# Cross-attention with a routed expert layer: attention in four steps of two head pairs, transposes and projection pieces in three shared PSUM banks

## The reference, cut to what matters

```python
# x, ctx: (32, 256, 256); mask: (32, 256); 16 heads of 64; 32 experts, hidden 64
h = layernorm(x)
q, k, v = h @ Wq, ctx @ Wk, ctx @ Wv
dots = q k^T * 64 ** -0.5, masked by mask and causally
x = x + softmax(dots) @ v @ Wo + bo
z = layernorm(x)
e = argmax(z @ router_w.T + router_b)          # one expert a token
x = x + relu(relu(z @ w1[e] + b1[e]) @ w2[e] + b2[e])
```

## Time and profile before

| | |
|---|---|
| median of the runs | 1570.09 us (1568.24 to 1631.78, 3 runs) |
| profiled execution | 1570.3 us, its span 1567.5 us |
| mean granted TensorE clock | 0.984 |
| instructions | 45480 |

### The profile page before, as it was taken

The page is one execution under the profiler, slowest core; times in us unless marked ns, Lnnn a source line. Parts: engine busy times, 40 slices in busy tenths (PEclk is TensorE's granted clock), DMA queues, the critical chain, the costliest instruction groups (busy, mean ns, idle before and its releaser), DMA issues.

```text
span 1567.5 us, 45480 instructions
## 1 busy us (share of the span) xinstructions
PE 1486.6 (95%) x14041; PEld 1248.9 (80%) x14042; DVE 1220.2 (78%) x5247; ACT 990.6 (63%) x3113; POOL 345.1 (22%) x508
## 2 busy tenths in 40 slices
PE   7899999999999999999999999999999999975884
PEld 6788888888888888888888888888888888864663
DVE  5777887888888888878888888888788888765663
ACT  5566666666666666666666666666666666643663
POOL 3212111111111111111111111111111111113776
PEclk9999999999999999999999999999999999997997
DMA  9543000000000000000000000000000000004761
GB/s 298 102 145 103 28 27 28 21 28 28 21 28 21 28 21 28 27 28 21 28 28 21 28 21 28 21 28 27 28 21 28 28 21 21 13 16 137 204 182 28
DMA packets 70399, 77.69 MB, mean 50 GB/s; under 512 B 11351, under 2 KB 64221, under 8 KB 70369
## 3 DMA queue, kind: packets, MB, share of 16 engines
q1 hardware_dynamic: 62546, 60.37, 14.0%
q0 software_dynamic: 7680, 16.93, 2.9%
q10 hardware_dynamic: 144, 0.03, 0.0%
HBM read 47.61 MB, written 33.88 MB: 52 GB/s over the span
## 4 chain that ended last, share of the span: by engine, by line
PE 81%; DVE 10%; issue 4%; ACT 1%; POOL 1%; DMA 1%; ACTq 1%; DVEq 0%; POOLq 0%; SPq 0%
PE psR L509 30%; PE psS L581 12%; PE psW L543 12%; PE psO L614 11%; PE psT L598 5%; PE psR L500 2%; PE psR L552 2%; DVE Sm L993 2%; DVE Sm L1010 2%; PE psS L1303 1%; PE psR L1293 1%; PE psT L1303 1%; DVE xn L830 1%; ACTq L1134 1%; PE psW L1282 1%
## 5 line engine op out<-in xcount | busy, mean ns | idle before, releaser
L739 ACT ACTIVATE Sm<-Sm,mneg 128x128 f32<-128x128 f32 (+1 forms) x1024 | 456.0, 449 | 364.1 <-DVE mneg L993 363.6
L993 DVE CUSTOM_DVE_ANT_0 Sm<-psS,MK 128x128 f32<-128x128 f32 (+1 forms) x1024 | 304.6, 354 | 110.4 <-PE psS L581 100.0
L581 PE MATMUL psS<-KT,QT 64*128 64x128 f32 (+1 forms) x2048 | 237.8, 351 | 21.0 <-DVE Sm L1010 18.6
L614 PE MATMUL psO<-PT,V 128*64 128x256 f32 (+1 forms) x2048 | 223.6, 339 | 1.3 <-ACT PT L730 1.3
L730 ACT ACTIVATE PT<-psT 128x768 f32<-128x768 f32 x256 | 204.5, 799 | 0.0
L581 PEld LDWEIGHTS psS<-KT,QT 64*128 64x128 f32 x2048 | 134.7, 187 | 77.9 <-issue 60.7
L739 ACT ACTIVATION_READ_ACCUMULATOR Sm<-Sm,mneg 128x1 f32 x1024 | 196.6, 192 | 0.0
L1010 DVE SCALAR_TENSOR_TENSOR Sm<-Sm,halve,rinv 128x512 f32<-128x512 f32 x256 | 193.3, 755 | 0.0
L448 POOL DMA_INDIRECT lists<-stg,lrow x64 | 67.8, 1059 | 560.0 <-DVE lrow L950 550.2
L614 PEld LDWEIGHTS psO<-PT,V 128*64 128x64 f32 x2048 | 124.5, 136 | 56.0 <-DVE OT_lo L1015 1.5
L598 PEld LDWEIGHTS psT<-ident,Sm 64*128 64x128 f32 x3072 | 138.2, 139 | 25.5 <-issue 1.7
(11 more groups left out here) (154 smaller groups left out, 2957.7 us busy)
## 6 DMA issues: line engine op xcount, KB each, us to landing
lists<-pad SPq DMA_DIRECT2D x8, 1560.0 KB, 12.9
XS<-lists SPq DMA_DIRECT2D x48, 260.0 KB
x_in<-in_x SPq DMA_DIRECT2D x32, 256.0 KB, 2.7
ctx_in<-in_ctx SPq DMA_DIRECT2D x32, 256.0 KB, 2.6
xr<-in_x SPq DMA_DIRECT2D x32, 256.0 KB, 2.6
W2R<-in_L_ffn_weights SPq DMA_DIRECT2D x1, 2048.0 KB
out<-Y,tok POOLq DMA_INDIRECT x96, 2.8
W2R<-in_L_xattn_Wv SPq DMA_DIRECT2D x2, 512.0 KB, 9.4
```

The costliest lines, as they stand in the source:

```text
L581: last = nc.tensor.matmul(psS[:, side, o:o + (it + 1) * P], QT[rows, p, it * P:(it + 1) * P], KT[rows, p, 0:(it + 1) * P], start=True, sto ...
L614: last = nc.tensor.matmul(psO[DH * side:DH * side + DH, t * P:N], V[:, t, DH * h:DH * h + DH], PT[:, blocks, :], start=(t == 0), stop=(t = ...
L739: nc.scalar.activation(v, v, ACT.Exp, bias=mneg[:, p % 2, k:k + 1], scale=-1.0, accum_out=rsum[:, p % 2, k:k + 1]).then_inc(s_exp, 1)
L993: nc.vector.tensor_tensor_reduce(out=Sm[:, p % 4, side, cols], in0=psS[:, side, cols], in1=MK[:, cols], scale=-SCALE, scalar=3e38, op0=ALU ...
```

## The change

A batch now has four steps, each for two pairs, a *quad*. In step s the PE does the scores of quad s+1 and the transposes of quad s, interleaved pair by pair, then the values of quad s-1 in one run of 16 instructions, then three to five pieces. psT, psW and the two psR banks are gone: psR has three banks, in which a quad's transposes lie (768 columns for each row half) and which the pieces then use in turn. psS has four banks, so that both pairs of a quad fit. Before the first transposes the PE waits for the reads of the last three pieces of the step before (`first_ready`), and it does so between the first and the second row block of the scores. A piece waits for the copy of the transposed probabilities from its bank, or for the read of the piece three before it.

The probabilities are copied in three parts of 512 columns into one of two buffers. `hi_o` and `lo_o` treat two pairs at once, 512 columns. The output projection is one piece, wo, at the end of step 0 of the next batch, in bank 2, and DVE reads it at the start of step 1. v2 is read by ACT instead of DVE. The router's stages are split: up to `tiles_run` in step 3 of the next batch, the rest in step 0 of the batch after that, and the rows are listed two batches later than their own instead of one. The mask's first-key scan is moved to step 0. In batch 0 DVE, not POOL, makes the low half of Wo. The first batches are written out for these offsets; the second phase only takes its banks from other names.

```diff
--- before.py
+++ after.py
...
-        PT = sb("PT", [P, 6, P])
+        PT = sb("PT", [P, 2, 3 * 512])
...
-        psS = ps("psS", 2)
-        psT = ps("psT", 2)
+        psS = ps("psS", 4)
         psO = ps("psO")
-        psW = ps("psW")
-        psR = [ps(f"psR{i}") for i in range(2)]
+        psR = ps("psR", 3)
...
+        QUADS = PAIRS // 2
+        PIECES = ((("v2", 0), ("xt", 1), ("wo", -1)),
+                  (("v3", 0), ("q0", 1), ("q1", 1), ("q2", 1)),
+                  (("x2", -1), ("k0", 1), ("lg", -1), ("k1", 1), ("v0", 1)),
+                  (("v1", 1), ("k2", 1), ("q3", 1), ("k3", 1)))
...
+            def iteration(b, prev, prev2, more, nxt=True):
+                if nxt:
+                    fold(b + 1)
+                if prev2:
+                    listed(b - 2)
+                if more:
+                    root1(b + 2)
+                if prev:
+                    root2(b - 1)
+                if nxt:
+                    lo_ctx(b + 1)
+                add_bias(b)
...
+            def scores(b, s, i, between=None):
+                p = 2 * s + i
                 for it, o in ((0, 0), (1, P)):
+                    if it and between:
+                        between()
                     for side in range(2):
                         rows = slice(DH * side, DH * side + DH)
-                        last = nc.tensor.matmul(psS[:, side, o:o + (it + 1) * P], QT[rows, p, it * P:(it + 1) * P],
+                        last = nc.tensor.matmul(psS[:, 2 * i + side, o:o + (it + 1) * P], QT[rows, p, it * P:(it + 1) * P],
                                                 KT[rows, p, 0:(it + 1) * P], start=True, stop=True)
                 last.then_inc(s_sc, 1)
 
+            def scores_may_start(b, s, first=False):
                 if not first:
+                    pe.wait_ge(s_sm, 8 * G(b, s) - 8)
+                pe.wait_ge(s_q, 4 * b + s + 1)
+                pe.wait_ge(s_k, 4 * b + s + 1)
+
+            def first_ready(b, s, prev, nxt):
+
+                pe.wait_ge(s_pn, 4 * G(b, s) - 2)
+                if s > 0:
+                    before = [(name, b + off) for name, off in pieces(s - 1, prev, nxt)]
+                elif prev:
+                    before = [(name, b - 1 + off) for name, off in pieces(QUADS - 1, prev, True)]
+                else:
+                    before = [(name, b) for name in FIRST]
+                if s > 0 or prev:
+                    pe.wait_ge(s_pt, 3 * G(b, s) - 3)
+                for name, at in before[-3:]:
+                    pe.wait_ge(*emptied(name, at))
+
+            def second_ready(b, s):
+
+                pe.wait_ge(s_pn, 4 * G(b, s))
+                pe.wait_ge(s_pt_half, G(b, s))
+
+            ring = psR[:].rearrange("p a n -> p (a n)")
+
+            def probs_t(b, s, i):
 
                 for side in range(2):
-                    for i, src in enumerate((2 * P, 0, P)):
-                        o = (3 * side + i) * DH
+                    for k, src in enumerate((2 * P, 0, P)):
+                        o = (6 * i + 3 * side + k) * DH
                         for h in range(2):
                             rows = slice(DH * h, DH * h + DH)
-                            last = nc.tensor.transpose(psT[:, h, o:o + DH], Sm[rows, p % 4, side, src:src + P],
-                                                       ident[rows, rows])
-                last.then_inc(s_pt_pe, 1)
-
+                            last = nc.tensor.transpose(ring[:, 768 * h + o:768 * h + o + DH],
+                                                       Sm[rows, 2 * (s % 2) + i, side, src:src + P], ident[rows, rows])
+                last.then_inc(s_pt_pe if i else s_pt_half, 1)
+
...
+                for s in range(QUADS):
+                    ahead = later(b, s + 1, nxt)
                     if ahead:
+                        if s == 0 and prev and not (isinstance(b, int) and b == 1):
+
+                            pe.wait_ge(s_pf, b - 1)
+                        scores_may_start(*ahead)
+                        scores(*ahead, 0, lambda: first_ready(b, s, prev, nxt))
+                        probs_t(b, s, 0)
+                        scores(*ahead, 1, lambda: second_ready(b, s))
+                        probs_t(b, s, 1)
+                    else:
+                        first_ready(b, s, prev, nxt)
+                        probs_t(b, s, 0)
+                        second_ready(b, s)
+                        probs_t(b, s, 1)
+                    if s > 0:
+                        values(b, s - 1, not prev and s == 1)
                     elif prev:
+                        values(b - 1, QUADS - 1)
+                    now = pieces(s, prev, nxt)
+                    for n, (name, off) in enumerate(now):
+                        if n < 3:
+                            pe.wait_ge(s_pt, 3 * G(b, s) - 2 + n)
                         else:
+                            pe.wait_ge(*emptied(now[n - 3][0], b + now[n - 3][1]))
+                        piece(name, b + off, psR[:, n % 3, :])
+                        if s == QUADS - 1 and prev and n == 1:
+                            ranks(b - 1, 8 * G(*ahead))
...
+            def probs_out(b, s):
+                act.wait_ge(s_pt_pe, G(b, s))
+                if not isinstance(b, int) or G(b, s) > 2:
+                    act.wait_ge(s_o_pe, G(b, s) - 2)
+                for k in range(3):
+                    nc.scalar.activation(PT[:, s % 2, 512 * k:512 * k + 512], psR[:, k, :], ACT.Copy).then_inc(s_pt, 1)
...
+            def hi_o(b, s):
+                act.wait_ge(s_o_pe, G(b, s))
+                if s == 0 and not (isinstance(b, int) and b == 0):
+
+                    act.wait_ge(s_wo_pe, b)
+                nc.scalar.activation(OTh[:, 2 * s:2 * s + 2, :].rearrange("p a n -> p (a n)"), psO[:, :], ACT.Copy
+                                     ).then_inc(s_o_hi, 1)
...
+                    exp(0, 0)
+                    probs_out(b, s)
+                    if s == 0:
+                        if prev:
+                            hi_o(b - 1, QUADS - 1)
+                            exp(0, 1)
+                            read("xt")
+                            exp(1, 0)
+                            exp(1, 1)
+                            read("v2")
...
+                    if s == 1:
+                        exp(0, 1)
+                        exp(1, 0)
+                        exp(1, 1)
+                        read("q0")
+                        if nxt:
+                            hi_ctx(b + 1)
+                        read("q1")
+                        hi_o(b, 0)
+                        read("q2")
+                    if s == 2:
+                        read("x2")
+                        exp(0, 1)
+                        exp(1, 0)
+                        read("k0")
+                        exp(1, 1)
+                        read("k1")
+                        hi_o(b, 1)
+                    if s == 3:
+                        exp(0, 1)
+                        exp(1, 0)
+                        exp(1, 1)
+                        read("k2")
+                        hi_o(b, 2)
+                        read("q3", "k3")
...
+                    if s == 0:
+                        route(prev2, b - 2, tiles_next)
+                        mask(0, 0)
+                        route(prev2, b - 2, rows_next)
+                        mask(0, 1)
+                        route(prev2, b - 2, rows_gap)
+                        mask(1, 0)
+                        route(prev2, b - 2, rows_near)
+                        mask(1, 1)
+                        if prev:
+                            lo_o(b - 1, QUADS - 1)
+                        route(prev2, b - 2, rows_all)
+                        if nxt:
+                            sum_ctx(b + 1)
+                        route(prev2, b - 2, rows_kept)
+                        norm(0)
+                        route(prev2, b - 2, row_places)
+                        read("xt") if prev else None
+                        route(prev2, b - 2, row_numbers)
+                        norm(1)
+                        route(prev2, b - 2, fills)
+                        if not prev:
+                            read("xt")
+                            lo_wo(0)
+                        if nxt:
+                            first_key(b + 1)
+                        if more:
+                            stats1(b + 2)
+                    if s == 1:
+                        if prev:
+                            residual(b - 1, bank_of(0, "wo", prev, nxt))
+                        mask(0, 0)
+                        mask(0, 1)
+                        mask(1, 0)
+                        mask(1, 1)
+                        norm(0)
+                        read("v3")
+                        if prev:
+                            stats2(b - 1)
+                        norm(1)
+                        lo_o(b, 0)
+                        if prev:
+                            apply2(b - 1)
+                        else:
```

(34 more changed lines are left out.)

551 lines of the change are left out of this document (241 added, 310 removed).

## The result

The changed kernel takes 1737.19 us in the median of four runs (1709.93 to 1764.8); the kernel before took 1569.16 us beside it (1567.69 to 1631.78). The ratio is 1.0901 [1.087, 1.0933], that is 1712 us against the 1570.09 shown ahead. The forecast was 1673 us with a range of 1595 to 1735. In some executions the second phase (the experts, which the change doesn't touch) runs at a granted clock of 0.50 and costs 54 to 66 us more, so the ratio compares executions without that, and the table of the experiments gives the two kinds apart.

What follows compares the result with a forecast made beforehand. The prediction took TensorE (PE, busy 95%) to bound the kernel. From 43.09 us a batch, less 2.0, plus 2.8 of stalls and 1.3 for each of two late readers, it got 46.5: 103 us more over 30 batches, 1673 us, range 1595 to 1735.

Steps and rivals of the forecast that it cites:

- Gain on PE, 2.0 us: On the PE, fewer changes between kinds of work and one wait gone: 2.0 us a batch saved, 41.1 if nothing waits.
- The bare edge: Between steps, PE waits for the last piece's read even if it starts at once: 0.61, 0.61, 0.70, 0.71, together 2.6 us.
- restarts: Each of the four PE stalls costs a further 0.05 us, making 2.6 into 2.8 us a batch.
- Two readers late by 1.3 each: Residual (step 1, held by list landing) and v0 copy (DVE's queue) start 1.3 us late; each stall becomes 2.0.
- The sum, 46.5 a batch: Period of one batch: 43.09 - 2.0 + 2.8 + 1.3 + 1.3 = 46.5 us, 3.4 more than before.
- the end, taken as even: Start and end of the run cost no net time, though the last batch's router work on DVE grows some 3 us.
- PE busy near 90% in the steady stretch, clock still 1.00: Sign expected in the steady attention stretch: PE busy share near 90%, TensorE's granted clock unchanged at 1.00.
- A: Rival: both readers start at once, only the unavoidable waits between steps remain; 43.9 us a batch, 1595 us; chance 0.15.
- B: Rival: only one of the two readers is late; 45.2 us a batch, 1634 us; chance 0.20.
- D: Rival: late residual delays masks and exps, making a third and fourth edge late; 49.1 us a batch, 1751 us; chance 0.09.
- C: Rival: waits between steps are hidden and saved transitions count; 41.1 us a batch, 1510 us; chance 0.06.
- The rule on rotating banks: Rotating PSUM banks overlaps evacuation with the next matmuls; by it the change is right inside a step, wrong at its edge.

Runs made afterwards that it cites:

- the last experiment: Changed kernel with VectorE's queue reordered and the shared-bank wait put behind both score row blocks of a pair: 1529.45 us, ratio 0.9745 to the kernel before.
- The run on DVE's order: Changed kernel with router stages, v0 read, first-key scan, layer norm parts and halving factor reordered on VectorE: 1598.14 us in one execution, 1663.42 in three with slow experts.
- The fillers: Changed kernel with eight unused identity matmuls where the PE would wait in steps 1 and 3: 1742.95 us, ratio 1.0701 to the kernel before.
- the second experiment: Changed kernel with lrow made before the first normalisation of step 0, so rows are listed earlier: 1721.24 us, ratio 1.0571 to the kernel before.
- the third: Changed kernel with rows listed earlier, and first-key scan and layer norm statistics moved from step 0 behind step 1's masks: 1709.7 us, ratio 1.0481 to the kernel before.
- the fourth: Changed kernel with the v0 read put right behind the second normalisation of step 2: 1727.67 us, ratio 1.0603 to the kernel before.

## Why the prediction was right and wrong

**Gain on PE, 2.0 us: right.** Values take 1.45 us per quad as forecast; the batch without low clock less its waits gives 41.1, the last experiment 41.3, the forecast 41.1.

**The bare edge, 2.6 and 0.2 for restarts: right as a wait and near as a sum, but by two errors that cancel.** The run on DVE's order has all four bare: 0.53, 0.59, 0.63 and 1.10, together 2.85 (2.8 forecast). The three copies cost less than their 0.61, 0.61 and 0.70, for the PE restarts 0.05 to 0.15 us after the reader's end and not 0.24, and nothing shows the further 0.05 for each restart. The residual costs 0.4 more than its 0.71, since it starts 0.45 us after the PE's last matmul and not 0.03. That the sum comes out is luck.

**Two readers late by 1.3 each: right in place and cause, sizes near.** The waits are 2.07 and 1.81 instead of 2.0 and 2.0. Less the bare edges of 1.10 and 0.63 the readers are late by 1.0 and 1.2. The residual is held by the landing of the list, shown by the second experiment (listed earlier, it starts earlier), and not by DVE, shown by the third; the v copy by what stands ahead of it on DVE, shown by the fourth. The third experiment also shows that the first-key scan and the statistics ahead of the residual cost nothing there.

**The sum, 46.5 a batch: 46.04 in the batches that it describes.** The missing term is TensorE's clock. The step that failed is the sentence "PE busy near 90% in the steady stretch, clock still 1.00", and with it a sum that prices a stall by its length alone. PE was busy 92% and the clock was 0.97, and the 1.58 us a batch that it costs (47.62 - 46.04) makes 47 us of the whole, a third of the 141 us that the change cost. The fillers show that the clock falls for the idle time: with the PE busy instead it stays at 1.00 and the slow groups are back at their length. Beside it the terms are: 46.5 to 46.04, 14 us less; the end, taken as even, 6 us more. 1673 + 47 - 14 + 6 = 1712, as the ratio gives. It lies inside the range of 1595 to 1735 because the range was made wide for rivals A, B and D; nothing in it was meant for the clock.

The Trainium skill (TensorE: Matmul & The Clock Gate, Part 1: The HAM clock gate) says that the clock has two levels, 1.2 and 2.4 GHz, and goes back to the lower one when the PE has been idle. The trace agrees in both: 0.50 from 615.00 to 617.00, 1.00 before, values of 2.36 us against 1.52, and 1.81 us of idle time ahead of it; it adds that the fall came 1.3 us after the PE was busy again. I had weighed no rule on the clock, since before its steady stretch was at 1.00 with no wait over 0.4 us; a new stall four to five times as long was outside what that stretch could vouch for, and one rival should have said so.

**The rivals.** A and B didn't come: both readers were late. C (1510 us, the edge hidden) was wrong for this code; with the wait later and DVE's order, where the edge is all but hidden, the time is 1529. D (1751) was nearest in time but not the mechanism: no third or fourth edge became late, the two on ACT being 0.53 and 0.59. The rule on rotating banks (the Trainium skill, Perfetto Trace Analysis, section Matmuls) holds here with a condition that the runs show: reading out overlaps only what the PE may still do ahead of the wait. With one score block there the three edges with a plain copy cost 0.5 to 0.6 us each; with both, some 0.4 us more, they cost nothing, and the residual's still 0.4.

**What stays open.** Why the tail is 6 us longer was not tried; PE's busy time in it is 3 us more at a clock of 0.88. Nor is it settled what decides whether a given stall lowers the clock, or why the residual starts 0.45 us behind the PE when nothing holds it.

## What to carry to other kernels

When two users of PSUM banks are put on one ring, write down what the matmul engine may still do in front of the common wait, and compare it with the whole way of the last bank: end of the matmul, copy, restart. Here, from the start of a piece's last matmul to the restart, it is 0.97 to 1.17 us for the three copies and 1.57 for the residual; behind one block of scores 0.5 to 1.1 us of it stays uncovered. Moving the wait behind one more block of scores, with the readers early in their engine's order, turned 9% slower into 2.5% faster. Price a stall of TensorE with what comes after it too (here from 1.54 us of idle time on), and look at the granted clock in narrow windows behind the longest idle time, not at its mean over the run.

## What the runs showed that I had not expected

- The clock can fall after the stall is over: at 613.58 the PE restarts at 1.00, from 615.00 on it is at 0.50 and fully busy, and stays there until after 617.00. The rows of the stall itself look clean; the damage stands in the next three groups.
- The length of the idle time alone doesn't decide. 1.54 us at the entry of step 3 left the clock up in 16 of 21 batches of the changed kernel; with step 1's stall cut to 1.0 us (8.0 / 8), the same 1.54 in step 3 (13.9 / 9) dropped it in every second batch. Taking away one stall moved half of the loss to the other. Some of the longest idle times of the changed kernel, up to 1.96 us, left the clock up, and in no run did a shorter one than 1.54 drop it in the steady stretch.
- A reader isn't just its copy. The residual, with DVE idle, starts 0.45 us after the matmul that it waits for, a v copy 0.04 after its own.
